# Small operands of the quantisation, an identity cast, 64 chunk differences and half of the residual moved in a decoder-layer kernel

## The reference

```
x = x + attention(layernorm(x), q, k, v, o weights and biases)
x = x + xattn(layernorm(x), fside, ctx)
x = x + ffn(layernorm(x), router, w1, b1, w2, b2)
```

```
ch_bias = (max over the chunk + min over the chunk) / 2      per channel
xz      = x - ch_bias
tmax    = max |xz| over chunk and channels; cmax = max |xz| per channel
scale   = tmax / 2^(7 - idx) / 7, idx from cmax against tmax / 2^k
result  = clip(round(xz / scale), -8, 7) * scale
y       = result @ dequantised W^T + ch_bias @ W^T + bias
```

## Time and profile before

| | us |
|---|---|
| median of 3 runs | 946.28 (946.28 to 946.4) |
| profiled execution, device time | 946.29 |
| its span | 944.6 |
| TensorE busy | 732.2 (78%) |
| VectorE busy | 745.5 (79%) |
| ScalarE busy | 594.7 (63%) |
| GpSimd busy | 150.5 (16%) |
| granted TensorE clock, mean | 0.885 |

### The profile page before, as it was taken

The page is one execution under the profiler, slowest core; times in us unless marked ns, Lnnn a source line. Parts: engine busy times, 40 slices in busy tenths (PEclk is TensorE's granted clock), DMA queues, the critical chain, the costliest instruction groups (busy, mean ns, idle before and its releaser), DMA issues.

```text
span 944.6 us, 15553 instructions
## 1 busy us (share of the span) xinstructions
PE 732.2 (78%) x5125; PEld 309.6 (33%) x5141; DVE 745.5 (79%) x1054; ACT 594.7 (63%) x1051; POOL 150.5 (16%) x253
## 2 busy tenths in 40 slices
PE   1557899999999999999955624565457279999997
PEld 0522332222222222222221123454336134444443
DVE  7899788999999999999989988888989864521111
ACT  4778545988988889889958025665438719651000
POOL 1200753011111121111220010000003130000010
PEclk9878997999999999999975857767768679999999
DMA  8600674122222222222140001110009520000000
GB/s 311 222 1 1 221 247 146 53 62 67 71 61 63 83 61 64 72 59 65 34 157 0 0 1 45 46 44 0 13 0 354 192 78 1 1 1 11 23 23 34
DMA packets 51598, 70.62 MB, mean 75 GB/s; under 512 B 13109, under 2 KB 27477, under 8 KB 51041
## 3 DMA queue, kind: packets, MB, share of 16 engines
q1 hardware_dynamic: 50272, 65.84, 21.9%
q0 software_dynamic: 1280, 4.20, 1.4%
HBM read 46.17 MB, written 19.12 MB: 69 GB/s over the span
## 4 chain that ended last, share of the span: by engine, by line
PE 49%; DVE 28%; ACT 10%; issue 7%; DMA 3%; POOL 1%; SPq 1%; ACTq 0%; POOLq 0%; DVEq 0%
PE PS L1513 12%; PE PS L1704 9%; PE PS L1715 9%; PE PS L1397 6%; PE PS L1530 6%; ACT slab L1831 4%; DVE slab L1093 2%; DVE slab L1111 2%; PE PS L1425 2%; ACT HB L1815 2%; DVE stats L749 2%; DMA slab<-in_x 2%; DVE slab L902 1%; DVE mx L1101 1%; DVE mx L1100 1%
## 5 line engine op out<-in xcount | busy, mean ns | idle before, releaser
L954 DVE TENSOR_REDUCE SWV<-PS 128x2 f32<-128x1024 f32 x256 | 300.8, 1214 | 15.3 <-PE PS L1397 14.1
L1831 ACT ACTIVATE slab<-PS 128x512 f32<-128x512 f32 x512 | 275.5, 595 | 35.3 <-PE PS L1530 27.7
L1513 PE MATMUL PS<-slab,HB 128*32 128x256 f32 x2048 | 164.0, 393 | 10.4 <-ACT HB L1815 10.4
L1530 PE MATMUL PS<-slab 50*128 50x512 f16 x512 | 125.9, 386 | 2.5
L1397 PE MATMUL PS<-slab 48*128 48x512 f16 x512 | 101.5, 392 | 1.8 <-ACT slab L1787 1.3
L1704 PE MATMUL PS<-slab 128*128 128x512 f16 x384 | 86.8, 390 | 1.4 <-DVE slab L1286 1.4
L1715 PE MATMUL PS<-slab 128*128 128x512 f16 x384 | 83.0, 379 | 0.0
L1513 PEld LDWEIGHTS PS<-slab,HB 128*32 128x32 f32 x2048 | 41.7, 108 | 90.6 <-issue 64.1
L1318 DVE SCALAR_TENSOR_TENSOR WOT<-PS,cmax,WOT 128x512 f32<-128x512 f32 x8 | 6.0, 751 | 69.8 <-PE PS L1715 69.8
L1312 DVE SCALAR_TENSOR_TENSOR slab<-HB,cmax,slab 128x512 f16<-128x512 f32 x32 | 23.9, 751 | 44.8 <-ACT slab L1924 44.8
L1397 PEld LDWEIGHTS PS<-slab 48*128 48x128 f16 x512 | 24.7, 93 | 102.1 <-issue 94.3
(11 more groups left out here) (306 smaller groups left out, 1143.7 us busy)
## 6 DMA issues: line engine op xcount, KB each, us to landing
slab<-in_L_ffn_w SPq DMA_DIRECT2D x2, 4096.0 KB, 14.1
q_split<-slab SPq DMA_DIRECT2D x24, 256.0 KB, 2.7
k_split<-slab SPq DMA_DIRECT2D x24, 256.0 KB, 2.7
slab<-q_split SPq DMA_DIRECT2D x64, 96.0 KB, 2.6
slab<-k_split SPq DMA_DIRECT2D x64, 96.0 KB, 2.6
slab<-in_x SPq DMA_DIRECT2D x4, 1024.0 KB, 12.2
slab<-HB SPq DMA_DIRECT2D x128, 32.0 KB
slab<-in_fside_BxS2xS SPq DMA_DIRECT2D x4, 1024.0 KB, 6.2
```

The source lines that it names most:

```text
L954: nc.vector.tensor_reduce(NM[:, ring].rearrange("p (a x) -> p a x", a=2)[:, :, x], PS[:, bank:bank + 2, :], AX.X, ALU.max, negate=True).th ...
L1513: ins = nc.tensor.matmul(PS[32 * h:32 * h + 32, 6, cols], VST[:, r % 2, k, h, :], PROB[:, k, h, cols], start=k == half == 0, stop=k == KB ...
L1530: nc.tensor.matmul(PS[:, st_bank(2 * s + a), :], KP[rows, r, p, P * k:P * k + P], QP[rows, r, p, :], start=True, stop=True).then_inc(st_re ...
L1831: nc.scalar.activation(PROB[:, k, 2 * a + p], PS[:, st_bank(t), :], ACT.Exp, scale=score_scale).then_inc(probs, 1)
```

## The change

The copy into CBX, the PICKS, the two `s0col` copies and AQ go from VectorE to GpSimd, behind its all-reduce. `cbt_ready` becomes two signals, and TensorE waits for both. VectorE and ScalarE wait for `ab_ready` instead. `identh` is cast at the front. The bias pass over chunks 0 to 63 of the second quantisation is done ahead of it, in two halves around the extremes of the last batch's third tile. Output tiles 4 to 7 and 12 to 15 are multiplied into a buffer OB of their own, and GpSimd adds them to X. The statistics of batch 1 move ahead of `prepare(0)`.

```diff
+        OB = slab[4][:, 0:4096].rearrange("p (t d) -> p t d", d=D)
+        POOL_TILES = [t for t in range(NT) if t // KB % 2]
...
             def quantise(k):
                 pool.wait_ge(tm_ready, k)
                 nc.gpsimd.partition_all_reduce(tmaxb[:, :], tm[:, :], P, RMAX).then_inc(tmax_ready, 1)
+                pool.wait_ge(cbt_scaled, k)
+                nc.gpsimd.tensor_copy(CBX[k - 1].rearrange("p c (b g n) -> p (c b) g n", b=B, g=4),
+                                      small["mn"][:, :].rearrange("p (c n) -> p c n", n=NC // B).unsqueeze(2).broadcast_to(
+                                          [P, CT * B, 4, NC // B])).then_inc(cbt_ready, 1)
+                for n, m in enumerate(((0, 1, 2), (3,))[k - 1]):
+                    ins = nc.gpsimd.tensor_scalar(PICKS[k - 1][n].rearrange("p (b g n) -> p b g n", b=B, g=4),
+                                                  s0i[0:4, :].rearrange("p (b n) -> p b n", b=B).unsqueeze(2).broadcast_to(
+                                                      [4, B, 4, NC // B]), identf[0:4, m:m + 1], None, ALU.mult)
+                ins.then_inc(cbt_ready, 1)
+                pool.wait_ge(cbt_ready, 2 * k)
+                for u in range(2):
+                    ins = nc.gpsimd.tensor_copy(s0col[64 * u:64 * u + 64, :],
+                                                s0[64 * u:64 * u + 64, :].rearrange("p (t u) -> p u t", u=2)[:, u])
+                if k == 1:
+                    own(ins)
+                    projection_scales()
+                else:
+                    ins.then_inc(ab_ready, 1)
+
+            def projection_scales():
+                for m in range(2):
+                    ins = nc.gpsimd.tensor_tensor(AQ[:, m], s0[:, :].unsqueeze(1).broadcast_to([P, CT, NC]),
+                                                  sw[:, m].unsqueeze(2).broadcast_to([P, CT, NC]), ALU.mult)
+                own(ins)
+                own(nc.gpsimd.tensor_scalar(AQ[:, 0], AQ[:, 0], qk_scale[:, 0:1], DH ** -0.5, ALU.mult, ALU.mult))
+                nc.gpsimd.tensor_scalar(AQ[:, 1], AQ[:, 1], qk_scale[:, 1:2], None, ALU.mult).then_inc(ab_ready, 1)
...
             quantise(2)
+            for n, t in enumerate(POOL_TILES):
+                pool.wait_ge(o_scaled, t + 1)
+                nc.gpsimd.tensor_tensor(X[:, t], X[:, t], OB[:, n], ALU.add).then_inc(x1_pool, 1)
             inv_std(0, 1, 2)
...
             own(nc.vector.tensor_copy(identb[:, :], identf[:, :]))
+            own(nc.vector.tensor_copy(identh, identf[:, :]))
...
+            def chunk_biases(lo, hi):
+                mx, mn, sc, cbias = (small[n][:, lo:hi] for n in ("mx", "mn", "sc", "cbias"))
+                own(nc.vector.tensor_tensor(sc, mx, mn, ALU.add))
+                own(nc.vector.tensor_scalar(cbias, sc, 0.5, None, ALU.mult))
+
+            def differences(lo, hi):
+                _, v = quantised(lo, hi)
+                own(nc.vector.tensor_tensor(v, v, bc(small["cbias"][:, lo:hi]), ALU.subtract))
...
-                nc.vector.tensor_copy(CBX[k - 1].rearrange("p c (b g n) -> p (c b) g n", b=B, g=4),
...
-                for n, m in enumerate(((0, 1, 2), (3,))[k - 1]):
-                    ins = nc.vector.tensor_scalar(PICKS[k - 1][n].rearrange("p (b g n) -> p b g n", b=B, g=4),
...
-                ins.then_inc(cbt_ready, 1)
...
-                for kind in PASSES:
+                for kind in PASSES[k - 1:]:
                     one_pass(kind, 0, Q_HALF)
-                for u in range(2):
-                    ins = nc.vector.tensor_copy(s0col[64 * u:64 * u + 64, :],
...
-                    own(ins)
                 bias_parts()
-                if k == 1:
-                    projection_scales()
+                dve.wait_ge(ab_ready, k)
...
             quantise(1, bias_parts)
-            nc.vector.tensor_copy(identh, identf[:, :]).then_inc(identh_ready, 1)
...
-            for c in range(2):
-                dve.wait_ge(norm_done, normalised_tiles(CT * (B - 1) + 2 + c))
-                extremes(B - 1, (0, 2)[c], (2, 1)[c])
+            dve.wait_ge(norm_done, normalised_tiles(CT * (B - 1) + 2))
+            extremes(B - 1, 0, 2)
+            chunk_biases(0, Q_HALF)
+            differences(0, Q_HALF // 2)
+            dve.wait_ge(norm_done, normalised_tiles(CT * (B - 1) + 3))
+            extremes(B - 1, 2, 1)
             dve.wait_ge(den_in, 32)
             nc.vector.reciprocal(RECIP_F, DENS_F).then_inc(rd_ready, 2)
+            differences(Q_HALF // 2, Q_HALF)
             dve.wait_ge(rb_mm, 1)
...
-            for t in range(NT):
-                dve.wait_ge(o_mm, t + 1)
-                if t >= 4:
-                    dve.wait_ge(x1_done, t - 3)
-                nc.vector.scalar_tensor_tensor(HB[:, t % 4], PS[:, t % 4], s0col[:, t:t + 1], SWO[:, :],
-                if t >= 2:
-                    residual(t - 2)
-            residual(NT - 2)
-            residual(NT - 1)
-            dve.wait_ge(x1_done, NT)
+            own_tiles = [t for t in range(NT) if t not in POOL_TILES]
+            for t in range(NT):
+                dve.wait_ge(o_mm, t + 1)
+                if t in POOL_TILES:
+                    dst = OB[:, POOL_TILES.index(t)]
+                else:
+                    n = own_tiles.index(t)
+                    dst = HB[:, n % 4]
+                    if n >= 4:
+                        dve.wait_ge(x1_done, n - 3)
+                nc.vector.scalar_tensor_tensor(dst, PS[:, t % 4], s0col[:, t:t + 1], SWO[:, :],
+                if t - 2 in own_tiles:
+                    residual(own_tiles.index(t - 2))
+            dve.wait_ge(x1_done, len(own_tiles))
             for b in (0, 2):
                 statistics(KB * b, KB * b + KB)
...
                 if n == 0:
+                    other_half_done(2 * KB)
                     statistics(3 * KB, 4 * KB)
...
             second_norm(0)
+            other_half_done(KB)
+            statistics(KB, 2 * KB)
             prepare(0)
-            statistics(KB, 2 * KB)
             second_norm(1)
...
             def chunk_bias(k, first, banks):
-                pe.wait_ge(cbt_ready, k)
+                pe.wait_ge(cbt_ready, 2 * k)
...
             def value_copy(u):
+                if u == 0:
+                    act.wait_ge(ab_ready, 1)
```

More of the change, by code:

```diff
@@ L332, in decoder_kernel @@
         qk_mm, qk_scaled, qk_h, qk_l = (sem(n) for n in ("qk_mm", "qk_scaled", "qk_h", "qk_l"))
-        bound_ready, bounds_ready, scale_ready, kp_ready, identh_ready = (
-            sem(n) for n in ("bound_ready", "bounds_ready", "scale_ready", "kp_ready", "identh_ready"))
+        bound_ready, bounds_ready, scale_ready, kp_ready, cbt_scaled = (
+            sem(n) for n in ("bound_ready", "bounds_ready", "scale_ready", "kp_ready", "cbt_scaled"))
         split_out = [sem(f"split_out{r}") for r in range(3)]
@@ L347, in decoder_kernel @@
         norm_done = sem("norm_done")
-        o_mm, o_scaled, x1_done = (sem(n) for n in ("o_mm", "o_scaled", "x1_done"))
+        o_mm, o_scaled, x1_done, x1_pool = (sem(n) for n in ("o_mm", "o_scaled", "x1_done", "x1_pool"))
         lw_in = [sem(f"lw_in{n}") for n in range(4)]
@@ L744, in weight, with other_half_done @@
                 nc.vector.reciprocal(swi[:, m], sw[:, m]).then_inc(sw_ready, 1)
+            def other_half_done(count):
+                dve.wait_ge(x1_pool, count)
             def statistics(lo, hi):
@@ L812, in chunk_bias_parts @@
                 ins.then_inc(cbp_ready, 1)
[L814 to L818, removed]
-                own(ins)
-                nc.vector.tensor_scalar(AQ[:, 0], AQ[:, 0], qk_scale[:, 0:1], DH ** -0.5, ALU.mult, ALU.mult).then_inc(ab_ready, 1)
-                nc.vector.tensor_scalar(AQ[:, 1], AQ[:, 1], qk_scale[:, 1:2], None, ALU.mult).then_inc(ab_ready, 1)
-                dve.wait_ge(ab_ready, 2)
             def scaled(u):
@@ L846, in bits @@
                     return s[name][:, :].bitcast(U32)
-                own(nc.vector.tensor_tensor(flat["sc"], flat["mx"], flat["mn"], ALU.add))
-                own(nc.vector.tensor_scalar(flat["cbias"], flat["sc"], 0.5, None, ALU.mult))
+                chunk_biases(0, CT * NC)
                 own(nc.vector.tensor_tensor(flat["mx"], flat["mx"], flat["cbias"], ALU.subtract))
@@ L868, in quantise @@
                 own(nc.vector.reciprocal(s0i[:, :], s0[:, :]))
-                own(nc.vector.tensor_tensor(flat["mn"].rearrange("p (c b n) -> p c b n", b=B, c=CT), over_channels(s["cbias"]),
-                                            s0i[:, :].rearrange("p (b n) -> p b n", b=B).unsqueeze(1).broadcast_to(
-                                                [P, CT, B, NC // B]), ALU.mult))
-                nc.vector.tensor_copy(CBX[k - 1].rearrange("p c (b g n) -> p (c b) g n", b=B, g=4),
-                                      flat["mn"].rearrange("p (c n) -> p c n", n=NC // B).unsqueeze(2).broadcast_to(
-                                          [P, CT * B, 4, NC // B]))
-                for n, m in enumerate(((0, 1, 2), (3,))[k - 1]):
```

(34 more changed lines are left out.)

2 lines of the change are left out of this document (removed).

## The result

The changed kernel takes 957.53 us (median of 4 runs, 956.83 to 959.1) against 946.28 before: 1.0131 times, 95% interval 1.0115 to 1.0146. It is slower by 11 to 12 us, where 8.65 us faster was forecast. Its profiled execution took 957.92 us.

A forecast was written before the change was run, and what follows sets the result against it. TensorE was taken to carry 49% of the chain and VectorE 28%. From 946.28 us, first quantisation -2.9, second -2.2, residual -1.8 and statistics -1.75 summed to -8.65, giving 937.6 us, range 932.8 to 942.5.

The forecast's parts named there:

- TensorE's start: First quantisation: chunk-bias matmuls wait for GpSimd's copy and picks, start about 65.5 instead of 64.23; 2.3 us cover, cost nothing.
- the start after 68: First quantisation: the prediction called itself wrong if TensorE's chunk-bias matmuls start after 68 us.
- the clock of 0.50: First quantisation: the prediction called itself wrong if TensorE's granted clock is 0.50 under the chunk-bias matmuls.
- Rival 3: First quantisation: GpSimd's picks get only gaps between VectorE's long passes, TensorE starts near 81; +4.6 us, 950.9; chance 0.05.
- Turns on the small instructions, +1.5: First quantisation: VectorE loses 1.5 us of GpSimd's 3.35 us of work by turn-taking during its twelve small scale instructions.
- GpSimd's prices: Small operands on GpSimd: copy 0.75 us, three picks and two s0col copies 0.24 each, AQ's four instructions 1.4; 3.35 in all.
- Identity cast, -2.06: First quantisation: the cast moved to the front costs nothing there, so TensorE's gapless run starts 2.06 us earlier.
- Differences, +2.4 for the last tile: Second quantisation: a 4.42 us pass leaves, but put into VectorE's holes it delays the last context tile by 2.4 us.
- Residual, -1.8: Output projection: VectorE's three adds after the last multiply go to GpSimd, saving 1.8 us.
- Statistics, -1.75: After the output projection: statistics moved from behind the roots into VectorE's idle time let the smoothing start 1.75 us earlier.
- the sum of -8.65: Whole kernel: -2.9 and -2.2 at the two quantisations, -1.8 residual, -1.75 statistics, together 8.65 us faster.
- the term for the turns, +2.2: Both quantisations: VectorE's loss to GpSimd's small-operand work, +1.5 us in the first and +0.7 in the second.

The follow-up runs named there:

- experiment 1: The changed kernel with the PICKS made by VectorE again; CBX, s0col and AQ stay on GpSimd: 934.73 us, 0.9905 of the kernel before.
- experiment 2: The changed kernel with GpSimd's PICKS as plain copies, without the multiplication (projection biases wrong, only times read): 935.86 us, 0.9914 of the kernel before.
- experiment 3: The changed kernel with one added wait: VectorE begins its long passes only when the PICKS are done: 947.92 us, 1.005 of the kernel before.
- experiment 5: The kernel before with the PICKS alone made by GpSimd, all else in place: 962.97 us, 1.0195 of the kernel before.
- experiment 6: The kernel before with single parts: identity cast 1.0005, differences 0.9993, residual 0.9971, statistics 1.0005; and unchanged once more, 1.0007.
- experiment 7: The changed kernel with PICKS on VectorE, run again: 935.06 us, 0.9899 of the kernel before; with AQ on VectorE too: 935.96 us, 0.9917.

## Why the prediction was wrong, step by step

- *"TensorE's start ... with some waiting about 65.5 ... I cost the delay at nothing."* This is the step that failed. It was 80.95. The sum priced the picks by their length alone, 0.24 each, and had no term for what GpSimd does between an all-reduce and its next arithmetic, though the trace had a pause of 7.59 us at just such a place, which ends with "issue" and not with an engine. Experiments 1, 2, 3 and 5 show it. Two of the prediction's own signs of being wrong came, the start after 68 and the clock of 0.50 under these matmuls.
- *Rival 3, starving picks.* The place, the turns as what holds the picks, and the start of TensorE (near 81) came out, at a chance of 0.05; what made the picks late enough to meet the passes it did not have. It was worked out as 950.9 and dismissed because GpSimd "has 5 us for 1.5 us of work"; the pause takes those 5 us. Its price was low by 6.6 us. TensorE's first bank ran at the low clock, 2.2 us more, VectorE waited 3.56 us in the second quantisation, and the cast brought less than 2.06.
- *Turns on the small instructions, +1.5.* Over-sized. In the changed kernel one instruction was stretched, by 0.40 us (0.18 to 0.58), but only the copy ran beside them; in experiment 2 copy, picks and s0col all did, and two were stretched, by 0.43 together (L910 0.59, L911 0.31). The turns do the damage the other way round: VectorE's 4.4 us passes hold GpSimd's tiny instructions. In experiment 1 they cost VectorE under 0.2 in two passes (4.51 and 4.50), where AQ's four instructions took over 10 us to get through.
- *GpSimd's prices.* Copy 0.61 (0.75 forecast), two s0col copies 0.42 (0.48), three picks as copies 0.90 (0.72), AQ's four behind the passes 1.76 (1.4): right in size.
- *Identity cast, -2.06.* At the front it takes 0.23, as forecast. The step "starts that run earlier" equated VectorE's saving with TensorE's: in experiment 6 VectorE's scaling came 2.1 us earlier, relative to the extrema, and TensorE's unit 5 only 0.9. The time alone is 1.0005; where the 0.9 went stays open.
- *Differences, +2.4 for the last tile.* From the start of ScalarE's last step of the attention loop to the last tile it was 7.2 us before and 9.8 in the changed kernel: +2.6, with GpSimd's product in front as forecast. The net of this part alone is -0.7 us (-1.9 to +0.5), forecast -2.0 without the small operands.
- *Residual, -1.8.* Held: no add stands behind the last multiply (550.65, then statistics at 551.32), measured alone -2.7 us (-4.2 to -1.1).
- *Statistics, -1.75.* The stretch shrank by 1.6; the whole time did not show it.
- With the picks back on VectorE, experiments 1 and 7 measure 0.990 of 943.5, -9.2 us, close to the sum of -8.65. That is in part luck: the cast and the statistics, -3.8 of the sum, did not show when measured alone, and the term for the turns, +2.2, was too large.

## What to carry to other kernels

A tiny instruction is not cheap on an engine where its kind is new: before moving one, look in the trace for that engine's idle time that ends with "issue", and ask which operation stood before it, and whether anything waits while it lasts. A small operand on which a long chain waits belongs on the engine whose result it follows at once; beside long two-input passes of VectorE, GpSimd's instructions get through at one per pass. And time saved ahead of another engine counts only up to that engine's own pause.

## What the runs showed of the hardware

- After a partition all-reduce, GpSimd's first arithmetic instruction (scalar or two-input) starts some 7 us late (7.10, 6.82, 7.59, 6.89, 7.14, 6.93 and 7.02 us above; 6.45 and 8.26 are the extremes in all traces here) where nothing else holds it up, while copies start at once, even in the same place from the same source. The pause begins with the sequencer's instruction ahead of the arithmetic, not always behind the all-reduce: it began after the copies when they came first, and where 32 us of waiting followed that instruction it did not show.
- The other way round, from arithmetic to an all-reduce, one place in each trace has an idle time that ends with "issue": 9.01 us at 37.23 above, 8.88 to 10.10 in all traces. At the quantisations GpSimd waits longer than that for VectorE anyway, or as long (8.95 in the kernel before).
- Beside VectorE's passes with two inputs in SBUF, three instructions of four partitions took 10.49 and 13.05 us, one per pass, against 1.78 with the passes held back; copies are held too (4.24 us for the two s0col copies beside a pass, 0.42 without). The Trainium skill, page "SBUF — State Buffer", section "Who interferes with whom", says that such instructions take turns whole; the traces agree.
